# Six running sums of slot attention on GpSimd, with its lists and banks reordered, and the matrix-memory stage with VectorE's work reordered

## The reference

```python
# block 1, slot attention (16 heads, 128 slots, 128 wide), scanned over the steps
Sk = Sk * gt[:, :, None, :] + k_t[..., :, None] * bw[:, :, None, :]
Sv = Sv * gt[..., None] + bw[..., None] * v_t[:, :, None, :]
s = einsum('bhd,bhdm->bhm', q_t, Sk) * SCALE
a = softmax(s, axis=-1)
o_t = einsum('bhm,bhmd->bhd', a, Sv)
# block 2, matrix memory (16 heads, 16 wide)
x = concatenate([q, k, v], axis=-1)
ig, fg = x @ Wi + bi, x @ Wf + bf
log_D = log_fg + ig;  D = exp(log_D - max_log_D)
C = (q @ k.T) / sqrt(dh) * D
Cn = C / (maximum(abs(C.sum(-1)), exp(-max_log_D)) + EPS)
h = Cn @ v;  hn = (h - mean(h)) * rsqrt(var(h) + EPS) * ln_scale
```

## Time and profile before

| | us |
|---|---|
| time, median of 3 runs | 5184.62 (5180.61 to 5185.2) |
| profiled execution, its own time | 5170.39 |
| profiled execution, span | 5168.4 |
| busy in the span: PE, DVE, ACT, POOL | 4929.0, 4247.0, 3752.5, 2158.3 |
| TensorE clock granted, mean | 0.982 |

### The profile page before, as it was taken

One profiled execution on the slowest core, in us unless ns is written; L12 is line 12 of the kernel. 1 busy time (PEld: TensorE's weight loads), 2 busy tenths in 40 slices (PEclk: granted clock), 3 DMA queues, 4 the chain that ended last, 5 costly groups with the idle time before them and its releaser, 6 DMA issues. The chain is left out here.

```text
span 5168.4 us, 113818 instructions
## 1 busy us (share of the span) xinstructions
PE 4929.0 (95%) x38150; PEld 3676.2 (71%) x38150; DVE 4247.0 (82%) x10304; ACT 3752.5 (73%) x9651; POOL 2158.3 (42%) x2776
## 2 busy tenths in 40 slices
PE   7999999999999999999999997879999989989999
PEld 4777777777777777777777776867856767778666
DVE  4999999999999999999999995879832268878523
ACT  4999999999999999999999984647823434446333
POOL 2555555555555555555555552431133300011432
PEclk9999999999999999999999998889999999999999
DMA  5500000000000000000000001010022373010224
GB/s 175 164 3 7 6 3 7 6 2 7 6 2 7 6 4 6 6 6 3 7 6 3 8 1 34 19 35 2 2 83 78 110 232 119 2 45 18 92 94 163
DMA packets 178112, 204.53 MB, mean 40 GB/s; under 512 B 28539, under 2 KB 165628, under 8 KB 176896
## 3 DMA queue, kind: packets, MB, share of 16 engines
q1 hardware_dynamic: 161840, 159.47, 10.1%
q0 software_dynamic: 12960, 34.63, 1.8%
q10 hardware_dynamic: 2736, 3.09, 0.2%
HBM read 158.33 MB, written 114.16 MB: 53 GB/s over the span
## 5 line engine op out<-in xcount | busy, mean ns | idle before, releaser
L471 ACT ACTIVATE sl<-PSA 128x512 f32<-128x512 f32 x58 | 34.6, 597 | 253.4 <-PE PSA L172 253.3
L274 DVE TENSOR_TENSOR hidden<-sl,PSA 128x512 f32<-128x512 f32 x60 | 41.2, 686 | 173.7 <-ACT sl L471 173.7
L1871 POOL TENSOR_TENSOR gsa_qka<-gsa_qka,gsa_tmpa 128x256 f32<-128x256 f32 x64 | 47.7, 745 | 315.7 <-DVE gsa_tmpa L1434 315.7
L1905 POOL TENSOR_TENSOR gsa_qkb<-gsa_qkb,gsa_tmpb 128x256 f32<-128x256 f32 x64 | 47.6, 744 | 306.8 <-DVE gsa_tmpb L1572 306.8
L1171 PE MATMUL PSA<-gsa_wo,gsa_sgb 128*128 128x256 f32 x512 | 129.3, 396 | 24.5 <-DVE gsa_r0b L1478 24.5
L1315 PE MATMUL PSA<-gsa_wo,gsa_sga 128*128 128x256 f32 x512 | 127.5, 392 | 25.1 <-DVE gsa_r0a L1611 25.1
L2404 POOL TENSOR_TENSOR mlstm_rs<-mlstm_wide,mlstm_neghalf 128x16 f32<-128x16 f32 x32 | 93.4, 2918 | 131.6 <-DVE mlstm_wide L2272 131.6
L1124 PE MATMUL PSA<-XT,gsa_wa 128*128 128x512 f32 x256 | 123.6, 606 | 8.0 <-DMA gsa_wa<-in_w_heads 7.6
L415 DVE COPY ffn0b_hT<-PSA 128x256 f32<-128x256 f32 x71 | 30.1, 424 | 122.7 <-PE PSA L213 122.7
L415 DVE COPY ffn1b_hT<-PSA 128x256 f32<-128x256 f32 x71 | 30.1, 424 | 121.6 <-PE PSA L213 121.6
L1171 PEld LDWEIGHTS PSA<-gsa_wo,gsa_sgb 128*128 128x128 f32 x512 | 93.1, 192 | 49.7 <-DVE gsa_r0b L1478 39.3
(11 more groups left out here) (854 smaller groups left out, 19165.1 us busy)
## 6 DMA issues: line engine op xcount, KB each, us to landing
pairs<-in_blank SPq DMA_DIRECT2D x2, 35904.0 KB, 128.1
ffn0b_XS<-pairs SPq DMA_DIRECT2D x71, 132.0 KB, 2.1
ffn1b_XS<-pairs SPq DMA_DIRECT2D x71, 132.0 KB, 2.1
gsa_wa<-in_w_heads SPq DMA_DIRECT2D x64, 128.0 KB, 2.1
X<-in_x SPq DMA_DIRECT2D x8, 512.0 KB, 8.0
mlstm_CX<-in_ctx SPq DMA_DIRECT2D x32, 128.0 KB, 2.0
ffn0b_WGU<-results SPq DMA_DIRECT2D x8, 512.0 KB, 4.8
ffn0b_WD<-results SPq DMA_DIRECT2D x8, 512.0 KB, 6.6
```

## The change

In gsa:
- The sixth addition goes to GpSimd, for both tiles; its semaphore counts 6 a pair now.
- The lists of all engines are reordered. A piece moves to an earlier call in several places: the projections of tile b, the turned sum of tile b, its maximum, and the residual of tile a now end the call of n - 1, not begin the call of n.
- VectorE: `early` stands ahead of `late` at level 1; decays of levels 4 and 16 stand between dependent convolutions; den2 stands behind both level products; -SCALE stands first in the call.
- GpSimd: the four masks of levels 4, 8, 32 and 16 stand in one row behind the second addition.
- PSUM banks are dealt out anew: the output matmul writes banks 2, 3 (6, 7) and waits for the gated product (onorm 1), not for r0 (onorm 3).

TensorE and VectorE first, then GpSimd, each for tile a; tile b is alike:

```diff
-                        pe.wait_ge(sum_a_by_dve, m * 1 + 1)
+                        pe.wait_ge(sum_a_by_pool, m * 6 + 6)
                         for j in range(4):
-                            last = nc.tensor.transpose(tile(PS[2], j), tile(QKa[:, 0:512], j), IDENT[:, :])
+                            last = nc.tensor.transpose(tile(PS[3], j), tile(QKa[:, 0:512], j), IDENT[:, :])
...
-                        pe.wait_ge(onorm_a_by_dve, m * 3 + 3)
+                        pe.wait_ge(onorm_a_by_dve, m * 3 + 1)
                         for j in range(4):
-                            last = nc.tensor.matmul(PS[1 + j // 2][:, (j % 2) * 256:(j % 2) * 256 + 256], tile(SGa[:, :], j), WO[:, :], start=True, stop=True)
+                            last = nc.tensor.matmul(PS[2 + j // 2][:, (j % 2) * 256:(j % 2) * 256 + 256], tile(SGa[:, :], j), WO[:, :], start=True, stop=True)
...
-                        dve.wait_ge(level_a_by_dve, m * 6 + 6)
-                        dve.wait_ge(sum_a_by_pool, m * 5 + 5)
-                        nc.vector.tensor_tensor(rights(QKa[:, 0:512], 32), rights(QKa[:, 0:512], 32), packs(TMPa[:, 1, :], 32), ALU.add).then_inc(sum_a_by_dve, 1)
...
+                        dve.wait_ge(packed_a_by_act, m * 12 + 10)
+                        nc.vector.tensor_tensor(late_end(GWVa[:, 0:1024], 16), late_end(GWVa[:, 0:1024], 16), late_ends_end(GWVa[:, 0:1024], 16), ALU.mult).then_inc(decay_a_by_dve, 1)
+                        nc.vector.tensor_tensor(early_end(GWVa[:, 0:1024], 16), early_end(GWVa[:, 0:1024], 16), early_ends_end(GWVa[:, 0:1024], 16), ALU.mult).then_inc(decay_a_by_dve, 1)
                         dve.wait_ge(conv_b_by_dve, m * 9 + 7)
...
+                        dve.wait_ge(slots_a_by_pe, m * 6 + 4)
+                        nc.vector.tensor_tensor(TMPa[:, 1, :], PS[1][:, 0:256], Ga[:, 3, :], ALU.mult).then_inc(level_a_by_dve, 1)
                     if earlier:
                         dve.wait_ge(onorm_b_by_pool, l * 2 + 1)
                         nc.vector.tensor_scalar(den2b[:, :], den2b[:, :], 1e-5, None, ALU.mult).then_inc(onorm_b_by_dve, 1)
...
+                        nc.vector.tensor_tensor(early(GWVb[:, 0:1024], 1), early(GWVb[:, 0:1024], 1), early_ends(GWVb[:, 0:1024], 1), ALU.mult).then_inc(decay_b_by_dve, 1)
+                        nc.vector.tensor_tensor(late(GWVb[:, 0:1024], 1), late(GWVb[:, 0:1024], 1), late_ends(GWVb[:, 0:1024], 1), ALU.mult).then_inc(decay_b_by_dve, 1)
...
                         nc.gpsimd.tensor_tensor(rights(QKa[:, 0:512], 2), rights(QKa[:, 0:512], 2), packs(TMPa[:, 1, :], 2), ALU.add).then_inc(sum_a_by_pool, 1)
...
+                        nc.gpsimd.tensor_tensor(packs(AMa[:, 2, :], 4), rights(CAa[:, :], 4), packs(MASKS[:, 2, :], 4), ALU.mult).then_inc(masked_a_by_pool, 1)
+                        nc.gpsimd.tensor_tensor(packs(AMa[:, 3, :], 8), rights(CAa[:, :], 8), packs(MASKS[:, 3, :], 8), ALU.mult).then_inc(masked_a_by_pool, 1)
+                        nc.gpsimd.tensor_tensor(packs(AMa[:, 5, :], 32), rights(CAa[:, :], 32), packs(MASKS[:, 5, :], 32), ALU.mult).then_inc(masked_a_by_pool, 1)
+                        nc.gpsimd.tensor_tensor(packs(AMa[:, 4, :], 16), rights(CAa[:, :], 16), packs(MASKS[:, 4, :], 16), ALU.mult).then_inc(masked_a_by_pool, 1)
...
+                        pool.wait_ge(level_a_by_dve, m * 6 + 6)
+                        pool.wait_ge(sum_a_by_pool, m * 6 + 5)
+                        nc.gpsimd.tensor_tensor(rights(QKa[:, 0:512], 32), rights(QKa[:, 0:512], 32), packs(TMPa[:, 1, :], 32), ALU.add).then_inc(sum_a_by_pool, 1)
```

```diff
-                    for k in range(2):
-                        for c in range(4):
-                            last = nc.tensor.matmul(PS[7][:, k * 128:(k + 1) * 128], WIF[:, c, k * 128:(k + 1) * 128], XC[n % KEPT][:, c, :], start=(c == 0), stop=(c == 3))
+                    for c in range(4):
+                        last = nc.tensor.matmul(PS[7][:, 0:128], WIF[:, c, :], XC[n % KEPT][:, c, :], start=(c == 0), stop=(c == 3))
...
-                    nc.vector.scalar_tensor_tensor(nd[b][:, :], H[b][:, :, 16], -1.0, ET[n // 4 % 2][:, n % 4, :], ALU.mult, ALU.max).then_inc(nd_by_dve, 1)
...
-                    nc.vector.tensor_tensor(nda[b][:, :], H[b][:, :, 16], nd[b][:, :], ALU.max).then_inc(nda_by_dve, 1)
...
-                    nc.vector.tensor_scalar(nde[b][:, :], nda[b][:, :], 1e-6, None, ALU.add).then_inc(nde_by_dve, 1)
+                    nc.vector.scalar_tensor_tensor(nde[b][:, :], size[b][:, :], 1e-6, ET[g % 2][:, n % 4, :], ALU.add, ALU.max).then_inc(nde_by_dve, 1)
...
-                    nc.vector.tensor_tensor(T1[b][:, :, :], T1[b][:, :, :], by_head(LNB[:, :]), ALU.mult).then_inc(weighed_by_dve, 1)
...
-                    nc.vector.tensor_tensor(rows(n), rows(n), T1[b][:, :, :].rearrange("p h d -> p (h d)"), ALU.add).then_inc(residual_by_dve, 1)
...
+                nc.scalar.preload_act_table_set("natural_log_exp_and_others")
...
+                    nc.gpsimd.tensor_tensor(T1[b][:, :, :], T1[b][:, :, :], by_head(LNB[:, :]), ALU.mult).then_inc(weighed_by_pool, 1)
...
+                    nc.gpsimd.tensor_tensor(rows(n), rows(n), T1[b][:, :, :].rearrange("p h d -> p (h d)"), ALU.add).then_inc(residual_by_pool, 1)
```

More of the change, by code:

```diff
@@ L1151, in pair @@
+                    if before:
+                        pe.wait_ge(level_a_by_dve, m * 6 + 3)
+                        pe.wait_ge(packed_a_by_act, m * 12 + 11)
+                        for e in range(2):
+                            last = nc.tensor.transpose(tile(PS[0][:, 0:256], e), tile(Pa[:, 5, :], e), IDENT[:, :])
+                        last.then_inc(turned_a_by_pe, 1)
+                        pe.wait_ge(level_a_by_dve, m * 6 + 4)
                         for e in range(2):
@@ L1234, in pair @@
                         last.then_inc(weights_a_by_pe, 1)
                         pe.wait_ge(level_b_by_dve, m * 6 + 1)
-                        for j in range(4):
-                            last = nc.tensor.transpose(tile(PS[7], j), tile(GWVb[:, 1024:1536], j), IDENT[:, :])
+                        for e in range(2):
+                            last = nc.tensor.matmul(tile(PS[4][:, 0:256], e), tile(LTb[:, 1, :], e), tile(AMb[:, 1, :], e), start=True, stop=True)
+                        last.then_inc(slots_b_by_pe, 1)
@@ new lines, in pair @@
+                        pe.wait_ge(reach_a_by_dve, m * 6 + 3)
+                        for e in range(2):
+                            last = nc.tensor.matmul(tile(PS[0][:, 0:256], e), tile(Pa[:, 1, :], e), tile(AMa[:, 1, :], e), start=True, stop=True)
+                        last.then_inc(weights_a_by_pe, 1)
+                        pe.wait_ge(values_b_by_act, m * 1 + 1)
+                        for e in range(2):
+                            last = nc.tensor.transpose(tile(PS[7][:, 0:256], e), tile(Pb[:, 3, :], e), IDENT[:, :])
@@ L1238, in pair @@
                         last.then_inc(turned_b_by_pe, 1)
-                        pe.wait_ge(reach_a_by_dve, m * 6 + 3)
+                        pe.wait_ge(weights_a_by_dve, m * 6 + 1)
+                        for e in range(2):
+                            last = nc.tensor.matmul(tile(PS[2][:, 0:256], e), tile(Pa[:, 2, :], e), tile(AMa[:, 2, :], e), start=True, stop=True)
+                        last.then_inc(weights_a_by_pe, 1)
                         if within:
@@ L1294, in pair @@
                     if before:
+                        pe.wait_ge(onorm_a_by_act, m * 1 + 1)
+                        for j in range(4):
+                            last = nc.tensor.matmul(PS[0][:, j:j + 1], tile(QKa[:, 0:512], j), ones[:, 0:1], start=True, stop=True)
+                        last.then_inc(read_a_by_pe, 1)
                         pe.wait_ge(level_b_by_dve, m * 6 + 3)
+                        pe.wait_ge(packed_b_by_act, m * 12 + 11)
+                        for e in range(2):
+                            last = nc.tensor.transpose(tile(PS[4][:, 0:256], e), tile(Pb[:, 5, :], e), IDENT[:, :])
@@ L1296, in pair @@
+                        last.then_inc(turned_b_by_pe, 1)
+                        pe.wait_ge(level_b_by_dve, m * 6 + 4)
                         for e in range(2):
```

766 lines of the change are left out of this document (383 added, 383 removed).

## The result

| | before | after |
|---|---|---|
| time, median of 4 runs | 5184.91 us | 5122.9 us (5115.13 to 5129.68) |
| profiled execution, its own time, span | 5170.39, 5168.4 us | 5123.26, 5121.6 us |

The ratio is 0.9876, with a 95% interval of 0.9864 to 0.9889: 64 us faster, where 28 were forecast. By the first and last instruction of each stage in the two traces, gsa takes 3049.5 us for 3088.7 (-39) and mlstm 271.9 for 298.2 (-26), together -65. The two spans differ by only 46.8 because `cross`, which is not touched, took 312 us in the traced execution, at a mean granted TensorE clock of 0.95, and 295 at 0.98 in that of before (1 is the level of 2.4 GHz, 0.5 that of 1.2). Whether it was long in the other three executions of the kernel after too, no trace shows.

The account below looks back on a forecast made before the run. VectorE was taken to bound gsa, TensorE right behind, both forming one loop in mlstm; gsa +13 and mlstm -41 summed to -28, 5184.6 to 5157 us. Range 5070 to 5222, 8 in 10; the forecast case alone 5130 to 5175.

Parts of the forecast that it names:

- I take VectorE for the bound, TensorE right behind it: gsa before: VectorE binds; its losses beyond about 1 us a pair, 47.3 to 46.3, make nothing faster.
- PE runs freely but for those two meetings: gsa before: TensorE's matmuls wait only twice a pair, 0.4 us each, for the last value of VectorE's norm.
- Added holds: gsa: VectorE stands still under GpSimd's operations in new places; with small pieces, +2.85 us a pair.
- beneath GpSimd's diagonal product: gsa, VectorE: level 1's reach, earlier by one operation, is held there, +0.3 us a half, +0.6 a pair.
- The level-1 `late`: gsa, VectorE: it no longer meets GpSimd's fourth addition, 0.41 us for 0.93, so -1.04 a pair.
- Case B: Rival, chance 0.24: meetings with GpSimd hardly happen, TensorE binds gsa at 46.27 us a pair; kernel at 5078 us.
- The new wait for the sixth sum: gsa: TensorE's transposition waits for GpSimd's later sixth addition; costed at nothing, or 0.5 us a half if uncovered.
- the addition's going: gsa: two sixth additions leave VectorE, 0.33 us each, -0.66 a pair.
- The rule that I set against the change: gsa: a two-input VectorE operation meeting a GpSimd SBUF read waits for the whole instruction; about two thirds was charged.
- Case C: Rival, chance 0.22: every new GpSimd meeting costs whole, both level-16 decays stopped, gsa +1.1 us a pair; kernel 5225 us.
- stops one decay once: gsa: a waiting operation slips between GpSimd's masks, so level 16's decays take one hit a half, +1.2 us a pair.
- The loop loses 1.4 of 7.81: mlstm: VectorE's work removed shortens each tile by 1.4 us; with the tail +2, -41 us.

Follow-up runs that it names:

- the version with den2 moved: Changed kernel with den2 put between the third and fourth level's product in both halves of gsa: 5026.9 us, ratio 0.971 against the kernel before.
- the tail on VectorE: Changed kernel with mlstm's ln_scale product and addition to X back on VectorE, behind widths: 6.87 us a tile, for 6.79 and 6.82.
- the run with the lighter VectorE: Changed kernel with VectorE adding only three of four output tiles of each half to X in gsa: a pair 45.39 us, for 46.74.

## Why the prediction was wrong

The direction was right, and the size was off twofold: 28 us forecast, 62 to 65 measured. The stages' errors are of opposite sign: gsa came out 52 us better than forecast (+13 against -39), mlstm 15 us worse (-41 against -26). A little of it is arithmetic: the recorded gsa terms add up to +0.15 a pair, which is +10 us and not +13, and those of mlstm to 1.34, not 1.4.

- **"I take VectorE for the bound, TensorE right behind it"** failed for the kernel before: taking 0.78 us from VectorE gave 0.30, and from TensorE 0.44. "PE runs freely but for those two meetings" rested on its matmuls' waits alone. VectorE was the bound only after the change, perhaps because TensorE's output matmul may now start on the gated product; no run takes that wait apart. VectorE's ledger adds up all the same, but what it gains in waits has to be read from both engines. I kept 0.22 us of VectorE's waits and forecast -0.5; all went, with the gaps around them, -0.99. This is the first mis-sized term, 0.5 us a pair or 31 us.
- **Added holds.** Their kind and place were right: mostly one hit for the two decays of level 16 (+1.06 for +1.2, of which 0.15 is the second hit in the fourth pair), den2 (+0.61 for +0.8). Level 1's reach "beneath GpSimd's diagonal product", +0.6, failed: measured +0.13, since the hold stood before already, on level 16's reach, 942 ns, and only changed its victim (L1528, 938 ns). This is the second term, 0.5 us. -SCALE went the other way, +0.47 for +0.14: I gave each half a hold of 0.36 and both took 0.5. The other small pieces took 0.3 more than forecast.
- **The level-1 `late`**, said to be free because `early` goes ahead: the size was right (-1.03), the reason half wrong: the order doesn't matter.
- **Case B's floor of 46.27** was wrong: TensorE does a pair in 45.4 or less. Its busy time is no floor. The forecast for B, 5078, is passed by the version with den2 moved.
- **The new wait for the sixth sum**, costed at nothing, cost nothing. But the addition's going, forecast at -0.66, gained nothing either, since -SCALE takes it back.
- **The rule that I set against the change** (the Trainium skill, "SBUF — State Buffer", "Who interferes with whom"), by which each meeting is paid whole, is borne out where an operation starts behind the start of a mask, an addition or a product of GpSimd's: den2 and -SCALE end within 0.03 us of GpSimd's end, and the decays of level 16 0.14 to 0.16 after a mask's. It isn't borne out for GpSimd's power, under which L1466 took its plain 0.41 us in nearly every pair. Case C, with both decays stopped by two masks, came in tile a in one pair of four. In the others, and in tile b (L1568, 282 ns), it did not, because the first decay starts 0.04 us ahead of the row. The prediction's reason against C, that a row of four masks "stops one decay once", is refuted; that C came in so few pairs was luck.
- **mlstm.** "The loop loses 1.4 of 7.81" failed: 1.02. Its largest part, 0.8 for two operations moved to GpSimd, was worth 0 to 0.2, and the table loads, which I costed at nothing since ScalarE "stays under", went with 0.3 to 0.6 a tile, a lower clock included. ScalarE's idle time was no cover: once in four tiles one load stands ahead of the logarithm and one ahead of the exp that the product waits for. I had charged the holds of GpSimd's operations in gsa and not here. The tail after the last piece grew by 5.5 us (12.7 for 7.2), for which I had 2; with the tail on VectorE it is 10.4.

What stays open: in mlstm, whether the granted clock makes the tile long or the waits bring the clock down, and which engines close its loop after the change; no run takes the absolute value, the fused gates' matmul or the statistics in twos apart.

## What to carry to other kernels

Where one engine's operations can stop another's, count as cost not only an operation's own duration but the holds that it makes and ends: an edit of 0.16 us was worth 1.23 a pair, and one of 0.66 nothing. Before summing savings on one engine, make it and its neighbour lighter by a known amount each; if both give a part, neither is the bound alone. Look at more than one pair before you call a hold absent: one pair of four had a second one. A table load in a dependent chain can be paid even on an engine that idles half the time, and a stretch is compared with another at the same granted clock.

## What the runs showed of the hardware that I had not expected

TensorE's busy share includes stalls that its matmuls' waits don't show: the same matmuls of a pair were busy 46.27 us before, 46.70 in the window above, and fit into 45.39 in the run with the lighter VectorE. -SCALE, an operation of VectorE on four columns, has a median of 0.67 us over the 64 pairs of the kernel after, in both halves, and of 0.18 and 0.24 us with den2 moved, where it is still held in 16 of the 64 pairs of tile a. Where two engines' lists are in step, a hold is met always, never, or in a fixed one of four pairs. At level 16's first decay a shift of 0.05 us decides over 0.57.
